# A fused window-attention and axial-attention block: Gram and axial output as 32x32 diagonal tiles, unrolled over the images

## The chip, the cores and the metric

The kernel runs on one core of a Trainium2 chip. The metric is the device time in microseconds. The median of three runs of the kernel before is 1061.59 us (1060.19 to 1064.38).

## The reference, cut to what matters

The input x is 32 images of 16x16 tokens with 256 channels, float32. Two layers follow each other, each with a residual:

```
x = x + window(gn(x))      # 8x8 windows, shifted by 4; 16 heads of 16 channels
x = x + axial(gn(x))

gn:     mean and variance over an image and 8 channels (32 groups)
window: q, k, v = xw @ Wq.T, xw @ Wk.T, xw @ Wv.T + bv
        q, k divided by their norm per head; logits = q k^T * scale + bias (+ mask)
        o = softmax(logits) @ v;  z = o @ Wo.T + bo
axial:  for a in (columns, rows):              # sequences of 16 tokens
            q, k, v = split(x @ w_qkv[a])      # 16 heads of 16 channels
            dots = q k^T / 16;  out_a = (dots @ v) @ w_out[a]
        result = out_0 + out_1
```

There is no softmax in the axial layer, so q (k^T v) gives the same: per sequence and head one 16x16 "Gram" matrix k^T v, and then q times it.

## The kernel before, in words

Channels lie on partitions in two groups of 128 (g), tokens along the free dimension, except where a stage needs tokens on partitions. Every float32 product that is done in float16 is done in three passes (`PASSES`): high*high, low*high, high*low. High parts are made by ScalarE (act.activation ... Copy), low parts by GpSimd (`low`, L955) or VectorE. So a projection of one 128-channel group over an image is 6 matmuls of 128x128 weights against 256 columns (`project`, L434 to L442).

One image passes through these stages: `image_channels` (transposes, TensorE), GroupNorm (`group_stats`, `group_moments`, `group_means`, `group_var`, `rstd`, `group_norm`), `window_qk`, `squares`, `window_norms` (L472, sums of squares per head by a matmul with a block matrix), `norm_logarithms` and `norm_reciprocals`, `scale_qk`, `window_v` (L490), `scores` (L517), `add_bias`, `probabilities`, `window_den` (L532), `window_pv` (L550), `window_out`, then for the axial layer GroupNorm again, `axial_kv` and `axial_q` (L439), `turn` (L1114, 32x32 transposes of k and v on VectorE, so that tokens come to partitions in blocks of 32), `kv_high`, `kv_low`, `widen_v` (L1122), `gram_matmuls` (L626), `gram_high` (L809), `gram_low` (L1135), `axial_out` (L649, L650), `o1_side`, `o1_sum`, `axial_y` (L666), `add_x1`, `result_rows`, `store_image`.

The two parts that the change is about, for each axis a:

- The Gram stage. After `turn`, a block of 32 partitions holds 32 tokens of two sequences for 32 channels. So the product wanted is block-diagonal: 4 blocks of 32 partitions. Before, SyncE copies k into `k_wide`, which is zero off these diagonal blocks (`spread_k`, 4 DMAs per image and axis, L390), and v is spread over two columns by a mask (`widen_v`). Then 16 blocks times 3 passes are 48 matmuls with 128x128 weights and 64 columns.
- The axial output. The Gram matrices are copied by SyncE into `gram_wide`, again zero off the diagonal blocks of 16 channels (`spread_gram`, 8 DMAs per image and axis, L382). Then 32 sequences times two are 64 matmuls with 128x128 weights, of 32 columns (high, both halves of q) and 16 columns (low).

The order of the work on each engine is written out by hand in its `step`: in step k TensorE works on images k to k-4 (SyncE on k to k-7). `over_steps` (L320) peels the first steps, runs a hardware loop (`Fori`) of four steps a pass, and peels the last ones; a pass of the loop ends in a branch on each engine. Engines wait for each other by semaphores: `reach` always waits, `edge` waits only where the image number is a Python integer, so not in the loop. TensorE's order in a step is: image_channels, window_norms, gram_matmuls(1), group_means(1), window_v, axial_y, axial_out(0), axial_kv(0), axial_q(0), group_means(0), scores(0), scores(1), axial_kv(1), axial_q(1), window_den, result_rows, axial_out(1), window_pv, gram_matmuls(0), window_qk, window_out.

Of the kernel before, what the change touches and what calls it, by code (L numbers as in the profile page):

```python
# [8 lines left out]
ALU = mybir.AluOpType  # L9
# [20 lines left out]
UNROLL = 4  # L30
# [12 lines left out]
def image(i, c):  # L43

    return Image(UNROLL * i + c, c % 2, UNROLL // 2 * i + c // 2, c % 4)


def earlier(img, by):
    return Image(img.n - by, (img.par - by) % 2, None, None)
# [6 lines left out]
def missing(n):  # L56
    return isinstance(n, int) and not 0 <= n < IMAGES
# [8 lines left out]
def is_first(img):  # L66
    return isinstance(img.n, int) and img.n == 0


def is_early(img):  # L70
    return isinstance(img.n, int) and img.n < 2


def edge(eng, sem, img, per=1, j=None):

    if isinstance(img.n, int):
        reach(eng, sem, img, per, j)


def constants():  # L80
# [10 lines left out]
    extra[:, 0], extra[:, 1], extra[:, 2], extra[:, 3] = LN_BIAS, np.log(8.0), -0.5, -0.5  # L91
    small = np.concatenate([halves, quad, odd, fourth, extra], 1)
# [11 lines left out]
def build(nc, x, Wq, Wk, Wv, bv, Wo, bo, logit_scale, cpb_w1, cpb_b1, cpb_w2, w_qkv0, w_out0, w_qkv1, w_out1,  # L104
          c_ident, c_group, c_heads, c_small, c_mask, c_coords, out, scratch):
    ctx = ExitStack()
    with ctx:
# [17 lines left out]
        minus_half = small[:, 44:46]  # L125
        bo_col = sb("bo_col", [P, G])
        bv_rows = sb("bv_rows", [P, G, D])
# [26 lines left out]
        kv = [sb(f"kv_{a}", [P, 2, G * BLOCKS, 32, 2], F16) for a in range(2)]  # L154
        k_wide = [sb(f"k_wide{a}", [P, G * BLOCKS, 4, 32, 2], F16) for a in range(2)]
        v_wide_both = sb("v_wide", [P, 2, G * BLOCKS, 2, 32, 2], F16)
        v_wide = [v_wide_both[:, a] for a in range(2)]
        gram = [sb(f"gram{a}", [P, G * SEQ, 2, DH, 2], F16) for a in range(2)]
        gram_wide = [sb(f"gram_wide{a}", [P, G * SEQ, 8, DH, 2], F16) for a in range(2)]
# [27 lines left out]
        wide_zeroed = sem("wide_zeroed")  # L187
# [19 lines left out]
        k_masked = sem("k_masked")  # L207
        v_ready = sem("v_ready")
# [19 lines left out]
        k_spread = [sem(f"k_spread{a}") for a in range(2)]  # L228
        v_widened = [sem(f"v_widened{a}") for a in range(2)]
        gram_done = [sem(f"gram_done{a}") for a in range(2)]  # L230
        gram_spread = [sem(f"gram_spread{a}") for a in range(2)]
# [13 lines left out]
        GN_STEPS = 10  # L245

        QK_BANK, NORM_BANK, V_BANK, DEN_BANK, PV_BANK, Z_BANK = 0, 4, 5, 1, 3, 7
        S_BANK, KV_BANK, Q_BANK = (6, 0), (3, 3), (5, 2)
        G_BANK, O_BANK, GM_BANK = (4, 6), (0, 6), (2, 3)
        Y_BANK, YT_BANK, XT_BANK = 2, 5, 3  # L250
        ZEROED = 4
# [7 lines left out]
        idle = v_wide_both[:].rearrange("p a x q e t -> p (a x q e t)").bitcast(F32)  # L259
# [1039 lines left out]
```

## Time and profile before

| | |
|---|---|
| median of 3 runs | 1061.59 us |
| profiled execution | 1066.87 us, its span 1064.8 us |
| instructions in the span | 43208, of these 18068 matmuls and 18068 weight loads |
| granted TensorE clock, mean | 0.972 |

The span is what lies between the first and last instruction of the profiled execution; all durations below are from it. PE is TensorE's matmuls and PEld its weight loads; each matmul of the program has one weight load ahead of it, and a float32 matmul is two matmuls with two loads. Durations of single matmuls include their way through the array, so they overlap; what a stage costs is told by the starts of the next ones in the timeline. "<-issue" stands where an engine sat idle and waited for nothing that the profile shows.

### The profile page before, as it was taken

To read this page: it belongs to the slowest core of one execution; us is meant where nothing else is said; L and a number is where in the kernel's file an instruction comes from. 1 tells how busy PE (TensorE), PEld (TensorE's weight loads), DVE (VectorE), ACT (ScalarE), POOL (GpSimd) and SP (SyncE) were. 2 spreads that over 40 slices of the span, in tenths; PEclk is the share of its full clock that TensorE was granted. 3 is DMA by queue.
4 is the path that set the end of the run, shared out by engine and by line. 5 is a ranking of instruction groups with operands and counts; after the bars stand their busy time and mean duration, and the time that the engine had idled before them with its cause. 6 is when DMAs were issued, how large, how long until landed. Compare 5 with 4: busy or idle time off the path is not lost.

```text
span 1064.8 us, 43208 instructions
## 1 busy us (share of the span) xinstructions
PE 969.7 (91%) x18068; PEld 832.4 (78%) x18068; DVE 852.4 (80%) x1684; ACT 611.9 (57%) x881; POOL 458.9 (43%) x329
## 2 busy tenths in 40 slices
PE   2468999999999989999899998999899999999874
PEld 2347888888888878888788987888788888888763
DVE  3658889888888888888788996888788888888841
ACT  2336566666666655666665664666456665666531
POOL 4123455344445453454444543454444444544430
PEclk9879999999999999999999998999999999999997
DMA  5102333333333332333333332333323333333332
GB/s 162 38 1 42 50 49 58 52 47 48 61 55 60 62 56 40 54 49 60 56 58 59 55 53 36 57 57 61 58 45 55 47 58 58 56 52 52 47 49 48
DMA packets 432682, 57.51 MB, mean 54 GB/s; under 512 B 413268, under 2 KB 431974, under 8 KB 432486
## 3 DMA queue, kind: packets, MB, share of 16 engines
q1 hardware_dynamic: 432486, 54.65, 31.2%
q8 instruction: 154, 2.52, 1.1%
q14 instruction: 42, 0.34, 0.1%
HBM read 12.63 MB, written 8.40 MB: 20 GB/s over the span
## 4 chain that ended last, share of the span: by engine, by line
PE 60%; SPq 11%; issue 9%; DVE 6%; POOL 4%; ACT 4%; DMA 4%; POOLq 0%; ACTq 0%; DVEq 0%
PE ps L439 27%; PE ps L626 6%; PE ps L649 4%; SPq L382 4%; PE ps L666 4%; PE ps L517 4%; SPq L390 3%; PE ps L472 3%; PE ps L550 3%; DMA gram_wide<-gram 3%; PE ps L650 2%; PE ps L532 2%; POOL kv L955 2%; PE ps L490 2%; PE ps L718 1%
## 5 line engine op out<-in xcount | busy, mean ns | idle before, releaser
L955 POOL TENSOR_TENSOR kv<-kv,kv 128x1024 f16<-128x1024 f32 x64 | 152.4, 2381 | 156.4 <-ACT kv L798 156.4
L798 ACT ACTIVATE kv<-kv 128x1024 f16<-128x1024 f32 x64 | 87.9, 1374 | 115.8 <-DVE kv L1114 115.8
L439 PE MATMUL ps<-xn,w_q 128*128 128x256 f16 x1152 | 143.7, 274 | 8.7 <-issue 8.7
L439 PE MATMUL ps<-xn,w_k 128*128 128x256 f16 x1152 | 144.7, 276 | 4.5 <-issue 4.0
L955 POOL TENSOR_TENSOR xn<-xn,xn 128x512 f16<-128x512 f32 x64 | 74.7, 1166 | 162.3 <-ACT xn L828 162.3
L960 POOL TENSOR_TENSOR stat<-stat,small 128x2 f32<-128x2 f32 x64 | 44.1, 690 | 207.3 <-DVE stat L1093 207.3
L439 PEld LDWEIGHTS ps<-xn,w_q 128*128 128x128 f16 x1152 | 111.2, 98 | 24.8 <-issue 11.6
L439 PEld LDWEIGHTS ps<-xn,w_k 128*128 128x128 f16 x1152 | 109.2, 99 | 20.0 <-issue 5.0
L626 PEld LDWEIGHTS ps<-v_wide,k_wide 128*128 128x128 f16 x3072 | 100.7, 98 | 29.9 <-issue 17.5
L649 PE MATMUL ps<-q,gram_wide 128*128 128x32 f16 x2048 | 111.5, 177 | 13.4 <-DMA gram_wide<-gram 13.4
L649 PEld LDWEIGHTS ps<-q,gram_wide 128*128 128x128 f16 x2048 | 108.2, 97 | 17.6 <-DMA gram_wide<-gram 16.8
L626 PE MATMUL ps<-v_wide,k_wide 128*128 128x64 f16 x3072 | 106.5, 194 | 8.3 <-DMA k_wide<-kv 6.2
L650 PE MATMUL ps<-q,gram_wide 128*128 128x16 f16 x2048 | 110.7, 170 | 0.0
L1197 DVE RECIPROCAL den_inv<-ps 128x512 f32<-128x512 f32 x32 | 107.3, 3352 | 2.9 <-PE ps L532 2.9
L650 PEld LDWEIGHTS ps<-q,gram_wide 128*128 128x128 f16 x2048 | 106.2, 97 | 0.5
L1135 DVE SCALAR_TENSOR_TENSOR gram<-ps,gram 128x1024 f16<-128x1024 f32 x64 | 85.2, 1332 | 21.5 <-ACT gram L809 20.6
L439 PE MATMUL ps<-xn,w_v 128*128 128x256 f16 x768 | 95.6, 275 | 0.0
L666 PE MATMUL ps<-o,w_o 128*128 128x256 f16 x768 | 91.9, 278 | 3.5 <-POOL o L955 3.5
L1114 DVE STREAM_TRANSPOSE kv<-ps 128x1024 f32<-128x1024 f32 x64 | 80.0, 1250 | 17.3 <-PE ps L439 17.0
L809 ACT ACTIVATE gram<-ps 128x1024 f16<-128x1024 f32 x64 | 83.7, 1308 | 10.8 <-PE ps L626 10.3
L666 PEld LDWEIGHTS ps<-o,w_o 128*128 128x128 f16 x768 | 76.3, 100 | 13.7 <-issue 3.6
L439 PEld LDWEIGHTS ps<-xn,w_v 128*128 128x128 f16 x768 | 75.8, 99 | 9.3
(110 smaller groups left out, 1928.0 us busy)
## 6 DMA issues: line engine op xcount, KB each, us to landing
k_wide<-kv SPq DMA_DIRECT2D x256, 64.0 KB, 2.3
gram_wide<-gram SPq DMA_DIRECT2D x512, 32.0 KB, 2.4
x_in<-x SPq DMA_DIRECT2D x32, 128.0 KB, 2.5
x_in<-x SPq DMA_DIRECT2D x64, 64.0 KB, 2.5
out<-y_out SPq DMA_DIRECT2D x32, 128.0 KB, 2.3
out<-y_out SPq DMA_DIRECT2D x64, 64.0 KB, 2.5
probs<-L_conv_w_qkv SPq DMA_DIRECT2D x1, 768.0 KB, 6.8
x<-L_conv_w_qkv SPq DMA_DIRECT2D x1, 768.0 KB, 8.5
```

The costliest lines, as they stand in the source:

```text
L439: last = pe.matmul(dst, w[:, wp, c, m * P:m * P + P], act[:, xp, c * TOK:(c + 1) * TOK], start=(n == 0), stop=(n == 5))
L626: last = pe.matmul(dst, k_wide[a][:, s, :, :, kp].rearrange("p q e -> p (q e)"), v_wide[a][:, s, :, :, vp].rearrange("p q e -> p (q e)"), ...
L649: pe.matmul(dst.rearrange("p (t i) -> p t i", t=2), high, q1[a][:, :, cols], start=True, stop=False)
L650: last = pe.matmul(dst[:, 0:SEQ], low, q1[a][:, 0, cols], start=False, stop=True)
L666: last = pe.matmul(ps[:, Y_BANK, g * TOK:(g + 1) * TOK], w_l1[a]["o"][:, wp, c2, g * P:(g + 1) * P], o1[a][:, xp, c2 * TOK:(c2 + 1) * TOK] ...
L798: act.activation(halves(kv[a][:], 0), kv32[a][:].rearrange("p t n -> p (t n)"), ACT.Copy).then_inc(kv_hi[a], 1)
L809: act.activation(gram_half(a, 0), ps[:, G_BANK[a]:G_BANK[a] + 2, :].rearrange("p b n -> p (b n)"), ACT.Copy, scale=GS / (WS * WS)).then_in ...
L955: return pool.tensor_tensor(dst, whole, high, ALU.subtract)
L960: pool.tensor_tensor(stat[layer][:, 28:30], stat[layer][:, 26:28], minus_half, ALU.pow).then_inc(gn_pow[layer], 1)
L1114: dve.transpose(dst, src).then_inc(kv_turned[a], 1)
L1135: dve.scalar_tensor_tensor(gram_half(a, 1), ps[:, G_BANK[a]:G_BANK[a] + 2, :].rearrange("p b n -> p (b n)"), GS / (WS * WS), gram_half(a, ...
L1197: dve.reciprocal(den_inv[:], ps[:, DEN_BANK, :]).then_inc(den_inverted, 1)
```

## The change

- `gram_matmuls` reads k directly: each 128x128 matmul becomes four of 32x32 weights on the diagonal (rows and output partitions 32q to 32q+31), in the same PSUM bank. `k_wide`, its zeroing and `spread_k` go.
- `axial_out` reads gram directly, in the same way: four 32x32 tiles each for high and low. `gram_wide` and `spread_gram` go. Since a 32-block holds two heads, gram itself must be zero between them: `gram_high` and `gram_low` now write it in two instructions each, with a mask as their scale.
- k, v and gram are laid out high part, low part, and no longer interleaved.
- `window_norms` and `group_means` use four diagonal 32x32 tiles in place of one 128x128 matmul.
- `spread_v` moves from VectorE to ScalarE; bv is no longer added to v but taken through Wo once (12 small matmuls at the first image) into the bias of the output.
- There is no hardware loop: all steps are written out. `edge` waits are given for the first and last 8 images alone.
- The PSUM banks are assigned anew, and the order of every engine's step is new. TensorE has six stages: k to k-5. Its order is: image_channels, result_rows, window_v, gram_matmuls(0), axial_out(1), group_means(1), axial_y, scores(0), axial_out(0), group_means(0), scores(1), axial_kv(1), axial_kv(0), window_den, window_qk, window_pv, window_norms, axial_q(0), gram_matmuls(1), axial_q(1), window_out.

```diff
-        def over_steps(eng, step, stages):
-
-            peeled = stages + 4
-            loops = (IMAGES - 2 - peeled) // UNROLL
-            for k in range(peeled):
-                step(0, k)
-            with eng.Fori(0, loops) as i:
-                for u in range(UNROLL):
-                    step(i, peeled + u)
-            for k in range(peeled + UNROLL * loops, IMAGES + stages - 1):
-                step(0, k)
+        def over_steps(step, stages):
+
+            for k in range(IMAGES + stages - 1):
+                step(k)
...
-            def spread_gram(a, img):
-
-                reach(sp, gram_lo[a], img)
-                for h in range(8):
-                    rows = slice(DH * h, DH * h + DH)
-                    sp.dma_start(gram_wide[a][rows, :, h].rearrange("p s e t -> p s (e t)"),
-                                 gram[a][rows, :, h % 2].rearrange("p s e t -> p s (e t)")).then_inc(gram_spread[a], 16)
-
-            def spread_k(a, img):
...
                 for t in range(2):
-                    last = pe.matmul(ps[:, NORM_BANK + t, :], head16[:], qk_sq[:, t, :], start=True, stop=True)
+                    for q in range(4):
+                        rows = slice(32 * q, 32 * q + 32)
+                        last = pe.matmul(ps[rows, NORM_BANK + t, :], head16[rows, rows], qk_sq[rows, t, :],
+                                         start=True, stop=True)
...
-                reach(pe, k_spread[a], img, 64)
+                reach(pe, kv_lo[a], img)
                 reach(pe, v_widened[a], img)
...
-                for s in range(G * BLOCKS):
-                    dst = ps[:, G_BANK[a] + s // 8, (s % 8) * 64:(s % 8) * 64 + 64]
-                    for n, (kp, vp) in enumerate(PASSES):
-                        last = pe.matmul(dst, k_wide[a][:, s, :, :, kp].rearrange("p q e -> p (q e)"),
-                                         v_wide[a][:, s, :, :, vp].rearrange("p q e -> p (q e)"),
-                                         start=(n == 0), stop=(n == 2))
+                for s in range(G * BLOCKS):
+                    for n, (kp, vp) in enumerate(PASSES):
+                        for q in range(4):
+                            rows = slice(32 * q, 32 * q + 32)
+                            last = pe.matmul(ps[rows, G_BANK[a] + s // 8, (s % 8) * 64:(s % 8) * 64 + 64],
+                                             kv[a][rows, 0, kp, 32 * s:32 * s + 32],
+                                             v_wide[a][rows, vp, s].rearrange("p q e -> p (q e)"),
+                                             start=(n == 0), stop=(n == 2))
...
                 for s in range(G * SEQ):
                     cols = slice(s * SEQ, (s + 1) * SEQ)
-                    dst = ps[:, O_BANK[a] + s // SEQ, (s % SEQ) * 2 * SEQ:(s % SEQ + 1) * 2 * SEQ]
-                    high, low = (gram_wide[a][:, s, :, :, gp].rearrange("p h e -> p (h e)") for gp in range(2))
-                    pe.matmul(dst.rearrange("p (t i) -> p t i", t=2), high, q1[a][:, :, cols], start=True, stop=False)
-                    last = pe.matmul(dst[:, 0:SEQ], low, q1[a][:, 0, cols], start=False, stop=True)
+                    at = (s % SEQ) * 2 * SEQ
+                    for q in range(4):
+                        rows = slice(32 * q, 32 * q + 32)
+                        pe.matmul(ps[rows, O_BANK[a] + s // SEQ, at:at + 2 * SEQ].rearrange("p (t i) -> p t i", t=2),
+                                  gram[a][rows, 0, s].rearrange("p h e -> p (h e)"), q1[a][rows, :, cols],
+                                  start=True, stop=False)
+                    for q in range(4):
+                        rows = slice(32 * q, 32 * q + 32)
+                        last = pe.matmul(ps[rows, O_BANK[a] + s // SEQ, at:at + SEQ],
+                                         gram[a][rows, 1, s].rearrange("p h e -> p (h e)"), q1[a][rows, 0, cols],
+                                         start=False, stop=True)
...
             def gram_high(a, img):
 
                 reach(act, gram_done[a], img)
-                reach(act, gram_spread[a], previous(img), 128)
-                act.activation(gram_half(a, 0), ps[:, G_BANK[a]:G_BANK[a] + 2, :].rearrange("p b n -> p (b n)"), ACT.Copy,
-                               scale=GS / (WS * WS)).then_inc(gram_hi[a], 1)
+                reach(act, o1_done[a], previous(img))
+                for h in range(2):
+                    last = act.activation(gram[a][:, 0, :, h, :], gram_sums(a, h), ACT.Copy, scale=gram_mask[:, h:h + 1])
+                last.then_inc(gram_hi[a], 1)
...
+            def spread_v(img):
+
+                reach(act, v_proj, img)
...
+                    for b in range(2):
+                        dst = v_diag[64 * b:64 * b + 64, half].rearrange("p t a d -> p (t a) d")
+                        last = act.activation(dst[:, :, DH * b:DH * b + DH], src[:, :, b, :], ACT.Copy, scale=1.0 / WS)
+                last.then_inc(v_ready, 1)
```

## Rows read from the trace of the kernel before

**Rows 1.** The page: busy time, share of the span, instructions of each engine
```profile
PE 969.7 (91%) x18068; PEld 832.4 (78%) x18068; DVE 852.4 (80%) x1684; ACT 611.9 (57%) x881; POOL 458.9 (43%) x329
```

**Rows 2.** Windows, 100 us each: busy of PE, PEld, DVE, ACT, POOL, PEclk, DMA, GB/s
```profile
400.00:500.00 100.00, 98.86 (x1854) 84.82 (x1854) 85.37 (x173) 62.92 (x92) 44.74 (x33) 0.99 0.32 51
```

**Rows 3.** The page's DMA queues: packets, MB, share of 16 engines
```profile
q8 instruction: 154, 2.52, 1.1%
```

**Rows 4.** Timeline of PE: start us, us, line, op, count [idle before <-releaser]
```profile
479.78 1.07 PE L532 MATMUL ps<-probs,small 128*32 128x256 f32 x16
...
503.77 1.57 PE L517 MATMUL ps<-qk,k_four 64*128 64x64 f16 x96
...
509.31 1.07 PE L532 MATMUL ps<-probs,small 128*32 128x256 f32 x16
...
510.80 0.18 PE L649 MATMUL ps<-q,gram_wide 128*128 128x32 f16 x1
...
512.39 0.17 PE L650 MATMUL ps<-q,gram_wide 128*128 128x16 f16 x1
512.49 1.10 PE L550 MATMUL ps<-probs,v_diag 128*32 128x64 f32 x64
513.52 1.84 PE L626 MATMUL ps<-v_wide,k_wide 128*128 128x64 f16 x48
515.30 1.47 PE L439 MATMUL ps<-xn,w_q 128*128 128x256 f16 x12
516.61 1.47 PE L439 MATMUL ps<-xn,w_k 128*128 128x256 f16 x12
...
522.89 0.65 PE L699 MATMUL ps<-ident,x_in 128*128 128x128 f32 x4 [3.50 <-issue]
523.37 1.88 PE L472 MATMUL ps<-qk_sq,head 128*128 128x512 f32 x4
525.09 1.61 PE L626 MATMUL ps<-v_wide,k_wide 128*128 128x64 f16 x48
```

**Rows 5.** Waits of PE: who waited <- for whom, us in total, times, longest
```profile
PE ps L699 <- issue: 14.2, 4, 3.7
PE ps L649 <- DMA gram_wide<-gram: 13.4, 11, 4.0
...
PE ps L626 <- DMA k_wide<-kv: 6.2, 6, 2.5
```

**Rows 6.** Timeline of PE in one stage, around 210 us
```profile
209.39 0.76 PE L550 MATMUL ps<-probs,v_diag 128*32 128x64 f32 x38
210.97 0.63 PE L550 MATMUL ps<-probs,v_diag 128*32 128x64 f32 x26 [0.82 <-issue]
```

**Rows 7.** DMA queue of instructions in 208.5:208.6 and in 212.5:212.6
```profile
q8 instruction: 1, 0.02, 57.9%
...
q8 instruction: 1, 0.02, 73.7%
```

**Rows 8.** The same in 603.7:603.8 and in 607:607.2
```profile
q8 instruction: 1, 0.02, 64.7%
...
q8 instruction: 1, 0.02, 32.2%
```

**Rows 9.** Timeline of PE: the norms after an idle of 3.74 us
```profile
398.86 1.11 PE L699 MATMUL ps<-ident,x_in 128*128 128x128 f32 x4 [3.74 <-issue]
399.76 2.93 PE L472 MATMUL ps<-qk_sq,head 128*128 128x512 f32 x4
```

**Rows 10.** Lines by form: busy us, mean ns | idle before <-releaser
```profile
L809 ACT ACTIVATE gram<-ps 128x1024 f16<-128x1024 f32 x64 | 83.7, 1308 | 10.8 <-PE ps L626 10.3
L816 ACT ACTIVATE o<-ps 128x512 f32<-128x512 f32 x64 | 38.1, 595 | 43.7 <-PE ps L650 43.7
L955 POOL TENSOR_TENSOR kv<-kv,kv 128x1024 f16<-128x1024 f32 x64 | 152.4, 2381 | 156.4 <-ACT kv L798 156.4
L1155 DVE SCALAR_TENSOR_TENSOR v_diag<-ps,bv_rows 64x256 f32<-64x256 f32 x128 | 53.7, 420 | 1.3
```

More of the change, by code:

```diff
@@ L56, in missing @@
 def missing(n):
-    return isinstance(n, int) and not 0 <= n < IMAGES
+    return not 0 <= n < IMAGES
 def reach(eng, sem, img, per=1, j=None):
@@ L717, in group_means @@
                 for h in range(2):
-                    last = pe.matmul(ps[:, GM_BANK[layer], 0:6].rearrange("p (g v) -> p g v", v=3), group8[:],
-                                     halves[:, :, h, :], start=(h == 0), stop=(h == 1))
+                    for q in range(4):
+                        rows = slice(32 * q, 32 * q + 32)
+                        last = pe.matmul(ps[rows, GM_BANK[layer], 0:6].rearrange("p (g v) -> p g v", v=3),
+                                         group8[rows, rows], halves[rows, :, h, :], start=(h == 0), stop=(h == 1))
@@ L720, in group_means, with step @@
                 last.then_inc(gn_sum[layer], 1)
-            def step(i, c):
-                for img in there(i, c):
+            def step(k):
+                for img in there(k):
                     image_channels(img)
-                for img in there(i, c - 1):
+                for img in there(k - 5):
+                    result_rows(img)
+                for img in there(k - 1):
+                    window_v(img)
+                for img in there(k - 3):
+                    gram_matmuls(0, img)
+                    axial_out(1, img)
+                for img in there(k - 2):
+                    group_means(1, img)
+                for img in there(k - 4):
+                    axial_y(img)
+                for img in there(k - 1):
+                    scores(0, img)
+                for img in there(k - 3):
+                    axial_out(0, img)
+                for img in there(k):
+                    group_means(0, img)
+                for img in there(k - 1):
+                    scores(1, img)
+                for img in there(k - 2):
+                    axial_kv(1, img)
+                    axial_kv(0, img)
+                for img in there(k - 1):
+                    window_den(img)
+                for img in there(k):
+                    window_qk(img)
+                for img in there(k - 1):
+                    window_pv(img)
+                for img in there(k):
@@ L726, in step @@
                     window_norms(img)
-                for img in there(i, c - 3):
+                for img in there(k - 2):
+                    axial_q(0, img)
                     gram_matmuls(1, img)
-                for img in there(i, c - 2):
-                    group_means(1, img)
-                for img in there(i, c - 1):
-                    window_v(img)
-                for img in there(i, c - 4):
-                    axial_y(img)
-                for img in there(i, c - 3):
-                    axial_out(0, img)
@@ L1281 @@
+                for img in there(k - 3):
+                    gram_low(0, img)
+                for img in there(k - 2):
+                    group_norm(1, img)
+            over_steps(step, 6)
 _INS = ["x", "L0_conv_Wq", "L0_conv_Wk", "L0_conv_Wv", "L0_conv_bv", "L0_conv_Wo", "L0_conv_bo",
```

526 lines of the change are left out of this document (258 added, 268 removed).

## The prediction

> **What bounds the kernel now.** I read the page first, then the windows, the timeline of TensorE, its waits, and last the DMA queues. TensorE is busy 91% of the span [rows 1], and in a stretch without fill and drain 98.9 of 100 us at the full clock, with VectorE at 85 [rows 2]. So it is TensorE's own stream that sets the pace. window_den of two images in a row starts at 479.78 and 509.31: 29.5 us an image [rows 4]. Four times the loop's branch costs about 3.6 us more, 14.2 in all, and waits for the two copying DMAs cost 13.4 + 6.2 us [rows 5]. 32 x 29.5 + 14.2 = 958 us, so 107 us are fill and drain.
>
> How much array time is a matmul worth? From the starts in [rows 4]: a projection takes 1.31 us per 12, 109 ns each. axial_out goes from 510.80 to 512.39 with 64 matmuls, 25 ns each, 1.6 us. A Gram stage is 48 in (1.61 - 0.19)/47, 30 ns each, 1.45 us. Scores, two row tiles side by side, go at (1.57 - 0.19)/95 = 14.5 ns; window_pv, four column tiles side by side, at (1.10 - 0.22)/63 = 14 ns. (0.19 and 0.22 are about what one matmul takes by itself.)
>
> The second limit is not on the page's first lines. In the middle of window_pv, between its 38th and 39th matmul, TensorE is idle 0.82 us for "issue" [rows 6]. No semaphore stands there, so it had no instruction. Instructions come by queue q8 in 154 packets of 2.52 MB / 154 = 16.4 KB [rows 3], that is 36136 / 154 = 235 matmuls and loads each, besides waits and what is fetched for nothing at branches; without the branches I take 250. One packet is in flight at 208.54 or so, TensorE resumes at 210.97, and the next packet appears at 212.5 [rows 6, 7]: 2.4 us from the packet to the resumption, 1.5 us to the next packet, 4.0 us a cycle. The packet is thus asked for only when the block before it is begun. Another pair of packets is 3.3 us apart [rows 8], without a stall. Before the change this hardly matters, as 250 instructions are an eighth to a quarter of an image.
>
> The Trainium skill ("Runtime: NRT & Kernel Launch", Instruction fetch mechanics) says that code comes in blocks of 256 instructions while the current one runs, and that crossing a block is mostly hidden; it gives TensorE room for 2048. By this rule the stall of rows 6 would not be there, and the change would cost no fetch time. The trace speaks against it; the rule's outcome is the first rival below.
>
> **The change part by part.** *Instruction count.* Per image a Gram stage had 48 matmuls and gets 192, twice; axial_out had 64 and gets 256, twice; norms 4 to 16, means 8 to 32. So 18068 / 32 = 565 pairs become about 565 + 288 + 384 + 12 + 24 = 1270, 2540 matmuls and loads, at 250 a packet 10.2 packets.
>
> *Array time.* If four diagonal tiles run side by side, as the four column tiles of window_pv do, a group of four takes the time of one 128x128 matmul: 26.7 ns of columns plus a little, with a pair per 7 ns. Gram stays 1.45 us, axial_out 1.7. Bounds: a gain of a few ns a group if the smaller weight load helps; and four times the time if they don't overlap (rival 3). I take no change. Norms: same columns, no change; means: 0.45 us may become 0.3, a gain of 0.3 an image. Array time of an image stays at 28 to 29 us.
>
> *Fetch time.* Now lay the new order of TensorE end to end. Gram(0), axial_out(1), means, axial_y, scores(0), axial_out(0), means, scores(1): 384 + 512 + 32 + 48 + 96 + 512 + 32 + 96 = 1712 instructions with 1.4 + 1.7 + 0.3 + 2.6 + 0.7 + 1.7 + 0.3 + 0.7 = 9.4 us of array time, but 6.8 packets. Then axial_kv twice, den, qk: 176 instructions, 8.7 us. Then pv, norms, q(0), Gram(1): 568 in 5.3 us, 2.3 packets. Then q(1), window_out, transposes and window_v: 104 in 4.8 us. A packet takes the longer of its array time and the fetch cycle. With cycle c, 10.2 packets cost 10.2 c, and more where a packet's own work is longer than c. The 8.7 us of the slow stretch mostly fall over two packets (176 of 250), about 3.5 us over; the 4.8 us stretch adds about 1.
>
> The cycle: below, it can't be under the 2.4 us from packet to resumption [rows 6, 7]; 3.3 us is the shortest distance in the dense part [rows 8]; above, 4.0 to 4.5, the stalled case. k_wide and gram_wide leave the DMA engines, so packets should be a bit quicker; I take 3.8. 38.8 + 3.5 + 1.0 = 43.3 us an image. With 3.0 it is 38, with 4.5 about 49, with 2.4 near 35.
>
> *No loop.* The 14.2 us of branches go, as do the waits of 19.6 us for the copies [rows 5]; late next is gram_low or kv_low, which TensorE no longer sees, since it comes 43 us later. The edge waits of the last and first 8 images are semaphore instructions in the stream, a few dozen.
>
> *The other engines.* v's four copies, 4 x 420 ns [rows 10], leave VectorE, and ScalarE gets four of 0.4 to 0.6 us, some 2 us an image. ScalarE has 612 / 32 = 19 us of 29.5 now [rows 1], of 43 then: hidden. gram_high in two of 595 ns each is no longer than the one of 1308; without interleaving, kv_low (2381 ns on GpSimd [rows 10]) can't be slower. VectorE's 26.6 us an image stay below the period. All of this hides behind TensorE; if TensorE kept its 29 us, VectorE with 25 us would still be below. SyncE loses 24 issues an image and no longer waits for gram and k; loading x and storing the result is all that is left.
>
> *Sum.* 32 x 43.3 = 1386, fill and drain 107, less about 10 of copy waits in it, plus about 10 for the sixth stage: 1493 us span, 1495 with the 2 us around it (1066.87 to 1064.8). The profiled run lay 0.5% over the median, so 1488; I say 1485.
>
> **The rivals.** (1) *Fetching is hidden* (the skill's rule, or packets that come several ahead in straight code). Then 29.5 less 0.3 and less 0.6 of copy waits and stalls: 28.7 x 32 + 107 = 1025 us, faster. For it: the average need, 10.2 packets of 16.4 KB in 29 us, is 6 GB/s, small beside the 51 GB/s that the queues move now [rows 2]. Against: the stall of rows 6 lies ahead of the loop, in peeled straight code. It decides if the cycle is under about 1.5 us, where 10.2 packets fit in 15 us and even the dense stretch nearly keeps up.
>
> (2) *The clock falls too.* After 3.74 us of idleness the four norm matmuls took 2.93 us in place of 1.88 [rows 9, 4]. In the dense stretches TensorE would work about 1 us and idle 2.8 in every cycle. If the clock falls in each of them, the slow stages behind run at half rate for some us: three to four times 1.5 us an image, 5 us, so 160 us more: 1640. For it: the same kind of gap; against: the gap at 519 to 522.89 us left the norms at 1.88 [rows 4].
>
> (3) *The four tiles don't run side by side*, since they are row tiles that write one PSUM bank. Scores have their two row tiles in two banks, so the trace has no case. Then a Gram group takes 4 x 29 in place of 29 ns, 96 times, and an output group 4 x 25, 128 times: 8.4 + 9.5 us more array time, in which fetching hides: 28.5 + 18 = 46.5 to 48, about 1630 us. The Trainium skill ("TensorEngine Tiling (Array Packing)", Gotcha 1) says that different row tiles can't access one PSUM bank at the same time. Here they write different partitions of it, of which that sentence says nothing; no row here shows it.
>
> **How the numbers follow.** Chances: forecast (fetch-bound, clock mostly kept) 0.67; clock falls as well 0.10; tiles don't overlap 0.06; fetch-bound but with a cycle under 2.7 us, 1150 to 1280, 0.06; hidden fetch, 0.11 (of it 0.01 within 0.5%, which is about what a measurement of this kernel can tell from no change). The forecast's own range is 1310 (c = 3.0) to 1660 (c = 4.5). For 8 in 10 I give 1270 to 1640. Faster 0.10, same 0.01, slower 0.89.
>
> **What would show it.** Right: over 320 packets in q8; PE and PEld with 2.2 times the instructions; busy share of PE down to about 70%; in the timeline pieces of Gram and axial_out broken by idle of 2 to 3 us "<-issue" every 125 or so matmuls; a period of 43 us from window_den to window_den. Wrong: Gram stages of 1.5 us without gaps (rival 1), single tiles 25 ns or more apart (rival 3), norms of 2.9 us or more and a low PEclk (rival 2). If the period is set by VectorE or a wait on a semaphore, the whole argument fails.

## The result and the profile after

The changed kernel takes 1641.8 us (median of 4 runs, 1634.0 to 1646.4), the kernel before 1060.9 beside it: a ratio of 1.543 [1.537, 1.548]. The direction and the fetching came out as forecast, the size did not: 1485 us were forecast. The time is 2 us above the 8-in-10 range (1270 to 1640) and inside the forecast's own range (1310 to 1660).

The page of the kernel after, in the order of [rows 1 and 3]: busy times, the granted clock in 40 slices, the instruction queue, and the chain that ended last by engine.

```profile
PE 1203.9 (73%) x40736; PEld 940.8 (57%) x40736; DVE 829.9 (50%) x1621; ACT 636.4 (39%) x1076; POOL 433.1 (26%) x325
...
PEclk8677877888768787778877778888878777877887
...
q8 instruction: 323, 5.29, 1.3%
...
PE 70%; issue 25%; ACT 3%; DVE 1%; POOL 0%; SPq 0%; DMA 0%; DVEq 0%; ACTq 0%; POOLq 0%
```

Read them against [rows 1 and 3]: 2.25 times the matmuls, 323 packets of instructions in place of 154, and no other engine near its limit. A quarter of the chain is "issue". The clock row is the second finding: it stands at 7 to 8 tenths almost everywhere, where the stretch of [rows 2] had 0.99. The profiled run had a mean granted clock of 0.79, the kernel before 0.97.

The longest waits of TensorE (us in total, times, longest), to be read against [rows 5]:

```profile
PE ps L651 <- issue: 135.3, 57, 3.1
PE ps L646 <- issue: 126.0, 63, 2.9
PE ps L618 <- issue: 97.7, 59, 2.7
```

L618 is the Gram stage, L646 and L651 the two matmuls of axial_out. Together 359 us in 179 pieces of 2.0 us: no semaphore is waited for; the queue of instructions below shows why. The copying DMAs of [rows 5] and the branch's wait are gone.

Windows of the kernel after (us; busy of PE, PEld, DVE, ACT, POOL with counts; PEclk, DMA share, GB/s): one image from norms to norms, and 100 us elsewhere, against [rows 2].

```profile
799.42:850.26 50.84, 37.07 (x1273) 29.13 (x1273) 25.77 (x51) 19.62 (x33) 13.48 (x10) 0.80 0.05 14
...
1000.00:1100.00 100.00, 81.00 (x2878) 64.63 (x2881) 58.56 (x116) 45.47 (x81) 29.13 (x21) 0.83 0.06 16
```

1273 matmuls an image (1270 were forecast). The same work takes 100 x 1273/2878 = 44 us in one place and 51 in another. VectorE's and ScalarE's 26 and 20 us an image are covered.

Timeline of TensorE through this image, as [rows 4]; of axial_out, whose groups of four stand one by one, only the rows at the stalls:

```profile
799.42 1.92 PE L443 MATMUL ps<-qk_sq,head 32*32 32x512 f32 x16
...
802.69 1.14 PE L618 MATMUL ps<-v_wide,kv 32*32 32x64 f16 x119
806.25 0.75 PE L618 MATMUL ps<-v_wide,kv 32*32 32x64 f16 x73 [2.43 <-issue]
...
811.84 1.28 PE L618 MATMUL ps<-v_wide,kv 32*32 32x64 f16 x136
814.64 0.61 PE L618 MATMUL ps<-v_wide,kv 32*32 32x64 f16 x56 [1.52 <-issue]
...
822.23 0.21 PE L646 MATMUL ps<-q,gram 32*32 32x32 f16 x4 [2.26 <-issue]
...
823.07 5.30 PE L669 MATMUL ps<-o,w_o 128*128 128x256 f16 x24
828.30 1.00 PE L492 MATMUL ps<-qk,k_four 64*128 64x64 f16 x48
829.23 0.20 PE L646 MATMUL ps<-q,gram 32*32 32x32 f16 x4
...
832.01 0.20 PE L651 MATMUL ps<-q,gram 32*32 32x16 f16 x3 [1.75 <-issue]
...
836.03 0.20 PE L651 MATMUL ps<-q,gram 32*32 32x16 f16 x3 [2.81 <-issue]
...
837.87 2.74 PE L407 MATMUL ps<-xn,w_k 128*128 128x256 f16 x12
840.40 2.40 PE L407 MATMUL ps<-xn,w_v 128*128 128x256 f16 x12
842.63 1.47 PE L407 MATMUL ps<-xn,w_k 128*128 128x256 f16 x12
```

Three readings. Inside a burst the tiles are fast: 119 in 1.14 us is (1.14 - 0.19)/118 = 8 ns each, 32 ns for the four that replace one matmul of 30 in the Gram stage. Each Gram stage is cut in two by an idle of 1.5 to 2.4 us in the middle of a loop without a semaphore. And after the bursts, full matmuls of other stages are slow: 24 of axial_y take 5.30 us (218 ns each), the projection at 837.87 takes 2.74 us where the one at 842.63, further from the stalls, has 1.47. A factor of two: that is the clock at its lower level, 1.2 in place of 2.4 GHz. The granted clock of these very stretches, the third number from the right, says so (axial_y and the projection at 842.63; from 837.87 to 840.40 it was 0.50 too):

```profile
823.07:828.30 5.23, 5.23 (x29) 3.45 (x26) 3.45 (x11) 1.08 (x2) 1.85 (x2) 0.50 0.01 3
...
842.63:844.10 1.47, 1.47 (x16) 1.32 (x14) 1.27 (x2) 0.00 (x0) 0.11 (x1) 1.00 0.06 11
```

The instruction queue of the kernel after in three stretches of 0.1 us, at 829.5, 833.6 and 837.5, as [rows 7 and 8]:

```profile
q8 instruction: 1, 0.02, 77.6%
...
q8 instruction: 1, 0.02, 54.8%
...
q8 instruction: 1, 0.02, 54.8%
```

4.1 and 3.9 us apart. TensorE resumes at 832.01 and 836.03, 2.5 and 2.4 us after the packets. Counted over the whole trace, TensorE has 195 pieces of over 0.7 us in which none of its recorded instructions (matmuls, loads, waits) starts. 173 of them stand at one and the same place of a block of 256 of these instructions. There it is 2.43 us in the median from packet to resumption (2.2 to 3.1), the next packet appears 1.2 us in the median after the resumption, and the 86 stalled cycles that follow one another directly take 3.75 us in the median (3.3 to 4.4).

For the runs below, each profile was cut the same way: the time from window_den of image 5 to that of image 25, by 20; of it the pieces of over 0.7 us from the start of one TensorE instruction to the start of the next, called idle; and the rest, which is array time and short gaps.

| kernel | us an image | idle over 0.7 us | rest |
|---|---|---|---|
| before | 30.7 | 1.3 | 29.4 |
| after | 48.7 | 12.7 | 36.0 |
| e1_unrolled | 29.5 | 0.1 | 29.4 |
| e9_unrolled_means | 29.3 | 0.1 | 29.2 |
| e2_one_full | 29.6 | 0.1 | 29.5 |
| e3_two_of_64 | 35.8 | 2.5 | 33.3 |
| e4_column_tiles | 47.9 | 12.4 | 35.5 |
| e5_five_passes | 56.5 | 17.2 | 39.3 |
| e7_more_columns | 46.4 | 8.7 | 37.7 |
| e8_norms_full | 48.7 | 11.9 | 36.8 |
| e10_in_halves | 47.8 | 9.7 | 38.1 |
| e12_three_in_halves | 46.6 | 10.4 | 36.2 |
| e11_full_interleaved | 39.3 | 5.0 | 34.3 |
| e6_interleaved | 63.8 | 4.5 | 59.4 |

In e6, e10 and e11 TensorE also waits for other engines, and the record of such a wait cuts a piece in two. From matmul to matmul the pieces are 5.9 us in e6, 12.0 in e10 and 8.4 in e11; for the others both counts agree within 0.1.

Before to after is 18 us an image: 11.4 of idleness, which is the fetching, and 6.6 of slower work. Where the 6.6 are, rows of single lines show. The projections are the same 144 matmuls an image in both kernels, the scores the same 96. Windows over these 20 images, busy of PE of one line each: in the kernel before L439, L490, L666 and the scores L517,

```profile
206.21:820.90 614.69, 246.00 (x2161) 0.99 0.34 54
206.21:820.90 614.69, 29.41 (x240) 0.99 0.34 54
206.21:820.90 614.69, 55.67 (x480) 0.99 0.34 54
206.21:820.90 614.69, 31.55 (x1920) 0.99 0.34 54
```

and in the kernel after L407, L461, L669 and L492:

```profile
288.95:1262.85 973.90, 290.20 (x2161) 0.81 0.05 14
288.95:1262.85 973.90, 29.47 (x240) 0.81 0.05 14
288.95:1262.85 973.90, 99.45 (x480) 0.81 0.05 14
288.95:1262.85 973.90, 46.44 (x1920) 0.81 0.05 14
```

331.1 us become 419.1, 4.4 an image, and the scores give 0.7 more. window_v (L461), which comes after other full matmuls, keeps its time; axial_y, right behind an output stage, pays 2.2 us an image. Together 5.1 us an image, 165 us over 32 images, of untouched work at the lower clock. (Against e2 below, which has the new order and no lower clock, the same four lines lose 4.8 us.) Most of the other 1.5 us is the tiles themselves: a group of four comes every 33 ns in the median of the whole trace, in place of one matmul every 30 ns in the Gram stage and every 25 ns in axial_out [rows 4]; for 96 and 128 groups an image that makes 1.3 us.

### The profile page after: what moved, and what is told of

Read it like the earlier page. It is cut to its first block, busy times and chain, and to the rows that moved or that the text cites. A ratio compares the mean times of both kernels' runs of the same rounds, so it can differ in the third digit from the quotient of the medians.

```text
span 1644.6 us, 87401 instructions
## 1 busy us (share of the span) xinstructions
PE 1203.9 (73%) x40736; PEld 940.8 (57%) x40736; DVE 829.9 (50%) x1621; ACT 636.4 (39%) x1076; POOL 433.1 (26%) x325
## 4 chain that ended last, share of the span: by engine, by line
PE 70%; issue 25%; ACT 3%; DVE 1%; POOL 0%; SPq 0%; DMA 0%; DVEq 0%; ACTq 0%; POOLq 0%
PE ps L407 28%; PE ps L669 10%; PE ps L618 7%; PE ps L646 6%; PE ps L492 4%; PE ps L443 4%; PE ps L651 4%; PE ps L461 2%; ACT qk_sq L844 2%; PE ps L507 2%; PE ps L720 1%; PE ps L686 1%; PE ps L700 1%; SPq L322 0%; DMA qk_sq<-L_conv_Wo 0%
## 5 line engine op out<-in xcount | busy, mean ns | idle before, releaser
L651 PE MATMUL ps<-q,gram 32*32 32x16 f16 x8192 | 157.3, 173 | 135.4 <-issue 135.3
L646 PE MATMUL ps<-q,gram 32*32 32x32 f16 x8192 | 158.8, 183 | 126.8 <-issue 126.0
L651 PEld LDWEIGHTS ps<-q,gram 32*32 32x32 f16 x8192 | 141.6, 93 | 139.2 <-issue 138.9
L646 PEld LDWEIGHTS ps<-q,gram 32*32 32x32 f16 x8192 | 141.7, 93 | 135.9 <-issue 132.8
L618 PE MATMUL ps<-v_wide,kv 32*32 32x64 f16 x12288 | 120.6, 192 | 100.7 <-issue 97.7
L407 PE MATMUL ps<-xn,w_k 128*128 128x256 f16 x1152 | 178.3, 317 | 0.0
L618 PEld LDWEIGHTS ps<-v_wide,kv 32*32 32x32 f16 x12288 | 108.3, 89 | 120.2 <-issue 117.9
L669 PE MATMUL ps<-o,w_o 128*128 128x256 f16 x768 | 159.5, 400 | 4.5 <-issue 4.3
L407 PE MATMUL ps<-xn,w_q 128*128 128x256 f16 x1152 | 155.4, 289 | 7.7 <-issue 6.3
L407 PEld LDWEIGHTS ps<-xn,w_q 128*128 128x128 f16 x1152 | 110.3, 102 | 64.3 <-issue 47.4
L407 PEld LDWEIGHTS ps<-xn,w_k 128*128 128x128 f16 x1152 | 126.8, 113 | 31.2 <-issue 0.3
L669 PEld LDWEIGHTS ps<-o,w_o 128*128 128x128 f16 x768 | 105.9, 141 | 48.3 <-issue 5.7
L979 POOL TENSOR_TENSOR qk<-qk 128x1024 f16<-128x1024 f32 x32 | 68.1, 2128 | 243.0 <-ACT qk L865 243.0
L1206 DVE TENSOR_TENSOR probs<-ps,bias_mask 128x1024 f32<-128x1024 f32 x64 | 78.3, 1224 | 85.3 <-PE ps L492 84.9
L1166 DVE SCALAR_TENSOR_TENSOR gram<-ps,small,gram 128x512 f16<-128x512 f32 x128 | 90.2, 746 | 47.5 <-ACT gram L813 47.3
L813 ACT ACTIVATE gram<-ps,small 128x512 f16<-128x512 f32 x128 | 80.8, 683 | 82.9 <-PE ps L618 82.7
## 6 DMA issues: line engine op xcount, KB each, us to landing
v_wide<-position_table SPq DMA_DIRECT2D x16, 28.2 KB
```

Source lines behind the costliest of these rows:

```text
L407: last = pe.matmul(dst, w[:, wp, c, m * P:m * P + P], act[:, xp, c * TOK:(c + 1) * TOK], start=(n == 0), stop=(n == 5))
L618: last = pe.matmul(ps[rows, G_BANK[a] + s // 8, (s % 8) * 64:(s % 8) * 64 + 64], kv[a][rows, 0, kp, 32 * s:32 * s + 32], v_wide[a][rows, v ...
L646: pe.matmul(ps[rows, O_BANK[a] + s // SEQ, at:at + 2 * SEQ].rearrange("p (t i) -> p t i", t=2), gram[a][rows, 0, s].rearrange("p h e -> p ...
L651: last = pe.matmul(ps[rows, O_BANK[a] + s // SEQ, at:at + SEQ], gram[a][rows, 1, s].rearrange("p h e -> p (h e)"), q1[a][rows, 0, cols], s ...
L669: last = pe.matmul(ps[:, Y_BANK, g * TOK:(g + 1) * TOK], w_l1[a]["o"][:, wp, c2, g * P:(g + 1) * P], o1[a][:, xp, c2 * TOK:(c2 + 1) * TOK] ...
L813: last = act.activation(gram[a][:, 0, :, h, :], gram_sums(a, h), ACT.Copy, scale=gram_mask[:, h:h + 1])
```

## The experiments

**Is it the number of instructions?** The theory: TensorE waits for blocks of instructions, whatever the tiles compute. The rival: 32x32 tiles in one bank are slow in themselves. Four runs.

e2_one_full: everything of the change stays (no loop, the direct reads, the copies on ScalarE, the tiles in norms and means), but in the Gram stage and axial_out one 128x128 matmul stands for four tiles.

```diff
-                        for q in range(4):
-                            rows = slice(32 * q, 32 * q + 32)
+                        for q in range(1):
+                            rows = slice(128 * q, 128 * q + 128)
```

> The kernel after with each group of four 32x32 matmuls in the Gram stage and the axial output made one 128x128 matmul on the same operands (it sums over all 128 partitions, so the products of the four blocks are mixed: the axial result is not the reference's). All else of the change stays: order, banks, v by ScalarE, no copies, no loop. 613 pairs an image. Fetch theory: 2.5 packets less 3.75 us each don't matter, the period is the array time of 28 to 29 us, clock at 1.0: 32 x 28.5 + 107 = 1020 us. Rival (the new order, the banks or ScalarE's added work cost the time): well over 1100 us, up to 1640.

Measured: 1028.1 us, ratio 0.968 [0.964, 0.971], 155 packets, clock 0.98. Two rows of its timeline, the Gram stage and axial_y:

```profile
801.99 1.56 PE L618 MATMUL ps<-v_wide,kv 128*128 128x64 f16 x48
...
811.62 2.78 PE L669 MATMUL ps<-o,w_o 128*128 128x256 f16 x24
```

The stage is whole and axial_y has its 2.78 us. So the whole loss of 614 us is in splitting these two stages, and everything else in the change together is a gain of 3%. By the table, an image loses 12.6 us of idleness and 6.5 us of slower work from e2 to the kernel after. Divided by the 168 packets more, 614 us are 3.7 us each; that this is near the cycle of 3.75 us is chance, since a third of the 614 us is not fetching.

e3_two_of_64: two tiles of 64x64 in place of four.

> As the one with full matmuls, but each group is two diagonal tiles of 64x64 (sums over 64 partitions, so again not the reference's result). 837 pairs an image, half-way in instructions. Fetch theory, packet by packet at 3.75 us: 31.5 us an image, 32 x 31.5 + 107 = 1115 us, with stalls of under 2 us and the clock mostly kept; to 1170 if the clock falls in part. Rival (tiles as such are slow, in proportion to their number): half of the way from the full to the 32x32 kernel, 1330 us.

Measured: 1209.0 us, 1.138 [1.128, 1.148], 211 packets, clock 0.92. It is over the range that I gave. From its timeline:

```profile
605.82 0.29 PE L720 MATMUL ps<-stat,group 32*32 32x6 f32 x9 [1.68 <-issue]
606.09 5.28 PE L669 MATMUL ps<-o,w_o 128*128 128x256 f16 x24
```

46% more matmuls than before (26400) give few stalls (2.5 us an image), but after a stall of 1.68 us axial_y already has 5.28 us: of the 5 us that an image loses, over half is not idleness. The granted clock was 0.50 from 606.09 to 611.20. The clock's part doesn't wait for the full change.

e4_column_tiles: as many instructions, but four column tiles of 128x32, each with all rows.

```diff
-                                             kv[a][rows, 0, kp, 32 * s:32 * s + 32],
-                                             v_wide[a][rows, vp, s].rearrange("p q e -> p (q e)"),
+                                             kv[a][:, 0, kp, 32 * s:32 * s + 32],
+                                             v_wide[a][:, vp, s].rearrange("p q e -> p (q e)"),
```

> The kernel after with the same number of matmuls, but each a column tile 128x32 (rows 0 to 127, output partitions 32q to 32q+31) as window_pv has them, in place of the diagonal 32x32 (sums over all partitions: not the reference's result). Fetch theory: the number of instructions decides, so the same time, 1600 to 1680 us. Rival (diagonal tiles in one PSUM bank hinder each other): clearly faster, 1300 us or less. Rival (clock falls because a diagonal tile uses a sixteenth of the array): faster by up to 200 us, since four times as much of the array works.

Measured: 1622.2 us, 1.527 [1.520, 1.534], 323 packets. It is 1% faster than the kernel after, the idle and the rest are 12.4 and 35.5 us in place of 12.7 and 36.0: the shape of the tiles is not what costs the time.

e5_five_passes: the tiles of the kernel after, two further passes in each Gram group.

```diff
-                    for n, (kp, vp) in enumerate(PASSES):
+                    for n, (kp, vp) in enumerate(PASSES + PASSES[1:]):
```

> The kernel after with two passes of the Gram stages repeated (five groups a block instead of three: 128 more 32x32 matmuls a Gram stage, 256 more pairs an image; the sums are then not the reference's). Fetch theory: 512 more instructions are 2 packets, at 3.75 us each 7.5 us an image, 235 us in all: 1880 us, with q8 at about 385 packets. Rival (array time decides): 64 groups of 29 ns, 1.9 us an image, 60 us: 1700 us.

Measured: 1892.8 us, 1.775 [1.768, 1.783], 387 packets: 64 packets and 251 us more, 3.9 us a packet. Most of what is added here is starved, so this is the direct test: the price of a further block of 256 instructions is about one cycle.

**Is the rest the clock?** Theory: the lower clock is what the forecast left out, and it comes with bursts of small tiles between idle pieces. Rival: the stages are slower for another reason, and the idle pieces are all that matters.

e7_more_columns: the same instructions, each tile streams 128 columns in place of 64, 32 or 16, so the array works longer in each block.

```diff
-                            last = pe.matmul(ps[rows, G_BANK[a] + s // 8, (s % 8) * 64:(s % 8) * 64 + 64],
+                            at = min((s % 8) * 64, 384)
+                            last = pe.matmul(ps[rows, G_BANK[a] + s // 8, at:at + 128],
```

> The kernel after with more work for the array and not one instruction more: every 32x32 matmul of the Gram stages and of the axial output streams 128 columns in place of 64, 32 and 16 (the output is not the reference's). Array time rises by 6 us an image, inside the idle of the fetch cycles. Theory (fetch cycle plus a clock that falls for lack of activity): a block of 128 matmuls then keeps the array busy some 1.9 of 3.75 us, the clock rises to above 0.9, and the time falls, to 1430 to 1520 us, though more is computed. Rival (fetch cycle is longer than thought, and the clock's part is small): the same time, 1640 us. Rival (array time counts in full): 1840 us.

Measured: 1561.6 us, 1.465 [1.459, 1.471], clock 0.95: more work in 80 us less. First the Gram stage and axial_y in its timeline, then the same four lines over 20 images (L407, L461, L671, L492):

```profile
807.35 2.07 PE L619 MATMUL ps<-v_wide,kv 32*32 32x128 f16 x133
810.15 1.01 PE L619 MATMUL ps<-v_wide,kv 32*32 32x128 f16 x59 [0.73 <-issue]
...
818.33 2.78 PE L671 MATMUL ps<-o,w_o 128*128 128x256 f16 x24
```

```profile
273.08:1200.75 927.67, 260.19 (x2161) 0.96 0.06 15
273.08:1200.75 927.67, 29.47 (x240) 0.96 0.06 15
273.08:1200.75 927.67, 64.60 (x480) 0.96 0.06 15
273.08:1200.75 927.67, 37.34 (x1920) 0.96 0.06 15
```

The projections are back at 354.3 of 20 images (331.1 before, 419.1 after), the scores at 37: 3.7 us an image regained, and the idle is 4.0 less, since the array works while the block comes. Against it stands what the wider tiles cost themselves, (2.07 - 0.2)/33 = 57 ns a group in place of 32. The clock's price of 5.1 us an image is confirmed by taking most of it away. The time came out above my range all the same. The wider tiles were priced about right: 224 groups at 25 ns more are 5.6 us an image, for the 6 that I expected. But not all of it went into the idle, which fell by 4.0 us, and 1.4 us of the clock's price stayed.

e6_interleaved: the stages of tiles and the projections are woven matmul by matmul, so that each block has long matmuls in it (`weave`, a merge of generators by their share done; the edge waits are given for every image, EDGE = 32).

```diff
+                while live:
+                    item = min(live, key=lambda x: x[1] / x[2])
+                    item[1] += 1
+                    if next(item[0], "end") == "end":
+                        live.remove(item)
```

> The kernel after with TensorE's order changed alone (and all edge waits given): Gram(0) is interleaved with window_v, axial_out(1) with axial_y, axial_out(0) with axial_kv(1), Gram(1) with axial_q of both axes, matmul by matmul in proportion. The number of instructions is the same, but each fetched block holds some long matmuls, so that the idle in a cycle is about 1.7 us and not 2.7. If the clock term is what separates 1642 from the 1485 of the fetch sum: the clock returns to above 0.95 and 10.3 packets at 3.75 us plus 1 to 2 us for the slow stretches that are left make 40 us an image, 1340 to 1400 us. If the clock doesn't depend on how the idle is spread (or the new order adds waits): 1550 us or more.

Measured: 2109.8 us, 1.979 [1.971, 1.987], clock 0.69, far worse than either expectation. One round of its timeline at either level of the clock, and the windows around them:

```profile
934.13 0.28 PE L707 MATMUL ps<-o,w_o 128*128 128x256 f16 x1
934.34 0.19 PE L683 MATMUL ps<-q,gram 32*32 32x32 f16 x4
934.38 0.17 PE L688 MATMUL ps<-q,gram 32*32 32x16 f16 x4
934.49 0.28 PE L707 MATMUL ps<-o,w_o 128*128 128x256 f16 x1
...
1001.94 0.21 PE L683 MATMUL ps<-q,gram 32*32 32x32 f16 x4
1001.99 0.18 PE L688 MATMUL ps<-q,gram 32*32 32x16 f16 x4
1002.10 0.39 PE L707 MATMUL ps<-o,w_o 128*128 128x256 f16 x1
1002.42 0.21 PE L683 MATMUL ps<-q,gram 32*32 32x32 f16 x4
```

```profile
933.77:934.90 1.13, 1.13 (x44) 0.69 (x36) 0.23 (x2) 1.09 (x3) 0.69 (x1) 1.00 0.22 56
...
997.81:1031.94 34.13, 30.55 (x742) 17.17 (x742) 8.49 (x19) 6.90 (x13) 3.96 (x5) 0.50 0.04 10
```

The long idle pieces for want of instructions are gone (0.35 us an image; the other 5.6 from matmul to matmul are waits for VectorE and ScalarE), as intended. But a round of 8 tiles and one full matmul takes 0.36 us at the full clock and 0.48 at the lower. From a full matmul's start to the next tile's it is 0.21 us at the full clock and 0.32 at the lower, though a full matmul is worth 0.11 and 0.22. So this change costs 0.10 us at either level, over the 20 images as in these rows. From the last group of tiles to the full matmul it is 0.10 to 0.12 us where a group takes 0.03. A pair of changes thus costs some 0.18 us, and an image has 82 of them: 15 us by this estimate. The Trainium skill ("TensorEngine Tiling (Array Packing)", Key Properties) says that a change of the tiling mode drains TensorE, with no figure. The trace agrees in direction.

The second window bears on the theory. The clock stood at its lower level for 34 us; in the 12 us before it fell the longest idle was 0.62 us, and in the window there is one wait of 3.09 us and else none over 0.32. So long idle pieces are not needed for the lower clock. Bursts between idle pieces are one case in which it fell, this mixture is another, and what both have in common was not tested.

e11_full_interleaved: the order of e6 with the full matmuls of e2.

> The interleaved order (matmul by matmul) with full 128x128 matmuls in place of the tiles, so that TensorE keeps one tiling throughout these stages and a third of the instructions goes (the axial result is not the reference's). Theory (changes between tilings are what made the interleaved kernel 470 us slower than after): 1030 to 1060 us, near the 1028 of the kernel with full matmuls in the order of after. Rival (the interleaved order itself, its waits or its single long matmuls between short ones): 1250 us or more.

Measured: 1328.0 us, 1.248 [1.239, 1.256]; the rival's outcome. Waits of TensorE in it:

```profile
PE ps L683 <- DVE probs L1236: 109.1, 30, 4.1
...
PE ps L428 <- ACT qk_sq L879: 49.3, 30, 1.8
```

The order of e6 costs 300 us against e2 with full matmuls, 9.7 us an image; 7.1 of these are waits for VectorE, ScalarE and GpSimd. So e6 is not a clean test: 300 us of it belong to the order, and the other 782 (24.4 us an image) to tiles among full matmuls. The changes of tiling are some 15 of these 24.4 us by the estimate above; most of what is left is the clock, which is at its lower level for 40 us an image in e6 and for 5 in e11 (from the mean granted clock over the 20 images).

e10_in_halves: the same order, but each stage in two halves, so that the tiling changes seldom.

```diff
-                    item = min(live, key=lambda x: x[1] / x[2])
+                    item = min(live, key=lambda x: int(2 * x[1] / x[2]))
```

> As the interleaved kernel, but each stage is cut in two only (half of Gram(0), half of window_v, the other halves, and so on), so that TensorE changes between tiles and full matmuls 14 times more an image than in the kernel after and not some 170 times. Theory (the interleaved kernel lost its time at these changes, about 0.3 us for each pair of them, and not to the fetch): 4 pairs more, 1 us; a block of instructions now holds 12 long matmuls or so, the clock stays at 0.9 or more, and the period is 41 to 44 us: 1350 to 1470 us. Rival (the clock doesn't depend on how the idle is spread): 1600 to 1700 us. Rival (the new order adds waits for VectorE, which are what the interleaved kernel lost): over 1750 us.

Measured: 1610.7 us, 1.514 [1.506, 1.522], clock 0.86. A miss: it carries the same waits of e11 (61.7 us for probs, 49.4 for qk_sq). It takes 500 us less than e6, from changing between tiles and full matmuls more seldom, and stays 2% under the kernel after in spite of these waits.

e12_three_in_halves: only three pairs of stages that are neighbours anyway are woven in halves, and no stage is moved.

> The kernel after with three pairs of neighbouring stages of TensorE cut into halves and alternated (Gram(0) with window_v, axial_out(1) with axial_y, Gram(1) with axial_q(1)); axial_out(0), axial_kv(1) and axial_q(0) stay where they are in after, since moving them is what brought the waits for VectorE and ScalarE in the kernel in halves. Same instructions. If the time depends on how the idle is spread (blocks with long matmuls in them have shorter idles, and the clock stays up more): 0.6 to 2.5 us less of slow array time an image, 1560 to 1620 us at a clock over 0.82. If not: 1635 to 1650 us, the kernel after's time, as the fetch sum is the same.

Measured: 1573.8 us, 1.476 [1.471, 1.480], clock 0.82: 68 us less than the kernel after. The time is in the expected range, but not for the expected reason: the idle is 10.4 in place of 12.7 us an image, while the rest, where slow array time would show, is 36.2 in place of 36.0. So weaving these three pairs returns a little, through the idle. That no other order returns more is not shown.

**The other parts.** e8_norms_full: the kernel after with norms and means as full matmuls again.

```diff
-                    for q in range(4):
-                        rows = slice(32 * q, 32 * q + 32)
-                        last = pe.matmul(ps[rows, NORM_BANK + t, :], head16[rows, rows], qk_sq[rows, t, :],
+                    last = pe.matmul(ps[:, NORM_BANK + t, :], head16[:], qk_sq[:, t, :], start=True, stop=True)
```

> The kernel after with one part undone: norms and means by full 128x128 matmuls, 36 pairs an image fewer. Fetch theory: 72 instructions are 0.29 of a packet, 1.1 us of fetch an image, less 0.3 us of array time that comes back at the means: 1610 to 1625 us. Rival (no effect on a kernel that is bound by the Gram and output stages alone): 1640 us.

Measured: 1657.7 us, 1.557 [1.546, 1.568]. The interval just meets that of the kernel after; 36 matmuls fewer an image bought nothing that shows: 0.8 us less idle and 0.8 more array time. A miss.

e1_unrolled: the kernel before, its loop written out, with nothing else of the change.

```diff
-            with eng.Fori(0, loops) as i:
-                for u in range(UNROLL):
-                    step(i, peeled + u)
+            for k in range(IMAGES + stages - 1):
+                step(k // UNROLL, k % UNROLL)
```

> The kernel before with its hardware loop written out and nothing else changed but that (edge waits for the first and last 8 images alone). Fetch theory: the instruction stream is as dense as before, 565 pairs an image, so no new stalls; the four idles at the branch (14.2 us) go and with them the slow clock behind some of them: 1040 to 1050 us. Rival (writing the loop out is itself what costs, since code is then read once and never again): over 1100 us.

Measured: 1038.1 us, 0.977 [0.974, 0.980]. A gain of 24 us, more than the 14.2 us of the branch's waits in [rows 5]: the idle over 0.7 us falls by 1.2 us an image, 24 us over 20 images, so shorter stalls in the loop go too.

e9_unrolled_means: e1 with the means on diagonal tiles.

> The kernel before without its loop (1038 us), and of the rest of the change only the diagonal tiles of group_means (32 in place of 8 matmuls an image, in stages that are not dense). The pace of the 16 small matmuls of after (0.40 us a stage against 0.51 to 0.59 before) gives 0.3 us an image: 1028 to 1035 us. Rival (24 more pairs push a fetch past the dense stage behind them): 1040 to 1050 us.

Measured: 1036.5 us, 0.973 [0.970, 0.975]. Just slower than the range given, and not told apart from e1 by the intervals. Both beat the kernel before and the one after. e2's 1028 us are no third, since its full matmuls mix blocks.

## Why the prediction came out as it did

*Instruction count and packets: right.* 1273 matmuls an image for 1270, 323 packets where over 320 were named.

*The fetch cycle: right.* 3.8 us taken, 3.75 measured, and e5 gives 3.9 us for each packet that is added. That a block is asked for when the one before it is begun fits the rows, in straight code too: the block begun at 836.03 lasts to 844.6, and its packet appears at 837.5. In 39 of the 322 blocks a second packet follows within the same block, so the fetching can run further ahead where TensorE is slow; the forecast had no such term. The Trainium skill says that crossing a block is "mostly hidden" ("Runtime: NRT & Kernel Launch", Instruction fetch mechanics). The traces of e1 and e2 agree, with 0.1 us of idle an image; the trace of the kernel after does not, where 256 instructions take about 1 us to execute. Rival 1 falls with e2 and e5.

*Tiles side by side: right.* 32 to 33 ns for four, forecast 28; this adds 1.3 us an image that the forecast put at nothing. Rival 3 is out: neither the shared bank (the kernel after) nor one row group (e4) matters. The Trainium skill ("TensorEngine Tiling (Array Packing)", Gotcha 1), weighed there, says that different row tiles can't access one PSUM bank at the same time; for diagonal tiles that write different partitions of one bank the trace shows no such cost, at 8 ns a tile.

*Idle of an image: nearly right.* The forecast had 43.3 - 28.2 = 15.1 us (28.2 is the sum of its four stretches); measured are 12.7 in pieces over 0.7 us.

*"Clock mostly kept": this step failed.* "Array time of an image stays at 28 to 29 us" came out as 36.0. The period is 48.7 in place of 43.3 us, 5.4 x 32 = 173 us more; fill and drain are 1644.6 - 32 x 48.7 = 86 in place of 107; together +152 us, which is the error. In the parts of the table, the rest is 7.8 us above the forecast's 28.2 and the idle 2.4 below its 15.1. Of the 7.8, the untouched projections and scores at the lower clock make 5.1, the pace of the tiles 1.3, and 1.2 stood in the kernel before already (29.4). This was rival 2, priced at 5 us and 1640 us in all and given a chance of 0.10. The argument against it was one gap of 3.50 us after which the norms kept 1.88 us [rows 4]; the argument for it was another that gave 2.93 [rows 9]. In the kernel before, such a gap came once in four images, and amid full matmuls. Here one follows on another, with 1 us of small tiles between them. Two gaps of the same length with different outcomes should have been read as "undecided", not as "kept". The sign named for rival 2 was only half right: the granted clock is low, but the norms keep 1.92 us (38.4 us in 20 images, as in e2), and the loss falls on axial_y, the projections and the scores. That 1642 us lies inside 1310 to 1660 is luck: the room at the top was left for a cycle of 4.5 us, and the clock filled it. What e3 adds: few gaps (2.5 us an image) are enough. What e6 adds: idles of 0.6 us can precede it too.

*No loop, and the other engines: right in sign.* e1 gives 24 us for the loop. VectorE, ScalarE and GpSimd stay hidden (gram_high takes two pieces of 683 ns, for which 595 were taken); e2 shows that they would have been hidden at 29.6 us an image too.

**Left open.** What e6 loses beyond its order (24.4 us an image) is split between changes of tiling and the clock by an estimate only. Why a group of four tiles takes 33 ns at the full clock with 16 and 32 columns (axial_out) as with 64 (Gram) isn't known. That e8 with fewer instructions isn't faster has no shown cause. What the hardware asks of TensorE to keep its clock was not measured; e6 shows that the absence of long idle pieces isn't enough.

## What to carry to other kernels

Before splitting a matmul into tiles, divide: 256 instructions took 3.75 us to arrive when TensorE was starved, so by this estimate a stage needs 15 ns or more of array time per instruction, 29 ns per matmul with its weight load, or enough slow work beside it. Tiles that go below that cost time. Here they were paid for twice, since full matmuls behind the stalls ran at the lower clock. Tiles woven among full matmuls one by one cost more still (e6). Writing a loop out costs nothing as long as the stages keep to that, and here gave 2.3%.

## What the runs showed of the hardware beyond that

- After stalls of 1.5 to 2.9 us between bursts of tiles, 24 full matmuls took 5.30 us in place of 2.78, at a granted clock of 0.50; with tiles of 128 columns and stalls of 0.7 to 1.7 us before them they kept 2.78 in the image shown (e7), at a granted clock of 1.00.
- Within an output stage the groups of four come 28 ns apart at first (nine from 829.23 in 0.25 us) and 33 ns later in the same burst (seventeen in 0.57 us); no run explains it.
- After a full matmul the first small tile came 0.10 us later than the matmul's own pace, at both levels of the clock (0.21 less 0.11 us, 0.32 less 0.22; e6).
- With tiles and full matmuls woven one by one the granted clock stood at 0.50 for 34 us, 13.6 of them (999.9 to 1013.5) without an idle piece over 0.3 us (e6).
